# High and low parts of the weighted sums made straight from PSUM, in two operations, in a fused two-layer kernel

## The reference, cut to what matters

```python
qz_u = qz @ ternary_factor_u.T * SCALE          # 16 channels of rank 64
qz_v = qz @ ternary_factor_v.T * SCALE
message_F = jnp.einsum('bcsr,bctr->bcst', qz_u, qz_v)
qh = jax.nn.sigmoid(message_F / REG_H)
qh_v1 = jnp.einsum('bcst,bctr->bcsr', qh, qz_v)
qh_v2 = jnp.einsum('bcst,bcsr->bctr', qh, qz_u)
...
message_G = (qh_v1 @ ternary_factor_u + qh_v2 @ ternary_factor_v) * SCALE
```

## Time and profile before

| | |
|---|---|
| median of 3 runs | 1738.5 us (1736.36 to 1742.24) |
| the profiled execution's own time | 1739.22 us |
| its span, first to last instruction | 1737.4 us |
| PE busy | 1578.7 us, 91% |
| DVE busy | 887.0 us, 51% |
| ACT busy | 826.6 us, 48% |
| granted TensorE clock, mean | 0.975 |

### The profile page before, as it was taken

One profiled execution on the slowest core, in us unless ns is written; L12 is line 12 of the kernel. 1 busy time (PEld: TensorE's weight loads), 2 busy tenths in 40 slices (PEclk: granted clock), 3 DMA queues, 4 the chain that ended last, 5 costly groups with the idle time before them and its releaser, 6 DMA issues.

```text
span 1737.4 us, 26600 instructions
## 1 busy us (share of the span) xinstructions
PE 1578.7 (91%) x8452; PEld 860.5 (50%) x8452; DVE 887.0 (51%) x1632; ACT 826.6 (48%) x1697; POOL 58.1 (3%) x45
## 2 busy tenths in 40 slices
PE   3399699999999899999999999999998999999977
PEld 1377564444445444454445444544555445544544
DVE  7868743334544454445443545445444544454447
ACT  2136235555555454545544554455554555455531
POOL 5000400000000000000000000000000000000000
PEclk9699799999999999999999999999999999999998
DMA  6002000000000000000000000000000000000000
GB/s 187 1 6 69 19 1 1 1 1 1 1 1 1 8 1 2 1 9 1 1 1 8 1 1 1 8 1 1 1 1 9 1 2 1 9 1 1 1 7 6
DMA packets 19945, 16.23 MB, mean 9 GB/s; under 512 B 1512, under 2 KB 18024, under 8 KB 19656
## 3 DMA queue, kind: packets, MB, share of 16 engines
q1 hardware_dynamic: 19448, 12.30, 2.6%
q0 software_dynamic: 336, 1.97, 0.3%
HBM read 9.94 MB, written 2.10 MB: 7 GB/s over the span
## 4 chain that ended last, share of the span: by engine, by line
issue 86%; DVE 6%; PE 6%; POOL 1%; DMA 1%; ACT 1%; SPq 0%; DVEq 0%; POOLq 0%; ACTq 0%
PE bank L1028 5%; DVE upper L514 1%; DMA x_all<-in_x 1%; DVE arena L734 0%; DVE arena L574 0%; DVE small L573 0%; DVE arena L740 0%; DVE upper L629 0%; DVE upper L627 0%; DVE upper L636 0%; DVE upper L638 0%; ACT arena L862 0%; DVE upper L625 0%; DVE upper L623 0%; DVE arena L732 0%
## 5 line engine op out<-in xcount | busy, mean ns | idle before, releaser
L952 ACT ACTIVATE arena<-bank 128x512 f32<-128x512 f32 x512 | 264.2, 602 | 205.4 <-PE bank L1028 205.2
L862 ACT ACTIVATE arena<-bank 128x512 f32<-128x512 f32 (+6 forms) x243 | 137.8, 585 | 337.3 <-PE bank L1165 183.1
L1028 PE MATMUL bank<-arena 128*64 128x512 f32 (+2 forms) x1280 | 282.2, 545 | 6.6 <-DVE arena L784 6.6
L952 ACT ACTIVATE th_high<-bank 128x512 f32<-128x512 f32 x512 | 264.5, 604 | 46.8 <-PE bank L1028 45.8
L682 DVE TENSOR_SCALAR arena<-bank,sums 128x512 f32<-128x512 f32 x128 | 96.1, 751 | 337.7 <-PE bank L1028 337.5
L1028 PE MATMUL bank<-th_high,arena 128*64 128x512 f32 x1024 | 247.9, 605 | 0.0
L1028 PE MATMUL bank<-u_parts,v_parts 64*128 64x512 f32 x1536 | 214.6, 409 | 16.7 <-ACT arena L952 11.3
L1028 PE MATMUL bank<-v_parts,u_parts 64*128 64x512 f32 (+1 forms) x1568 | 221.1, 408 | 0.0
L1028 PEld LDWEIGHTS bank<-v_parts,u_parts 64*128 64x128 f32 (+1 forms) x1568 | 140.2, 184 | 70.8 <-issue 45.8
L1028 PEld LDWEIGHTS bank<-u_parts,v_parts 64*128 64x128 f32 x1536 | 134.7, 184 | 79.7 <-issue 38.9
L938 ACT ACTIVATE arena<-bank 128x512 f32<-128x512 f32 x130 | 77.8, 598 | 174.3 <-PE bank L1028 128.2
(11 more groups left out here) (179 smaller groups left out, 1718.0 us busy)
## 6 DMA issues: line engine op xcount, KB each, us to landing
x_all<-in_x SPq DMA_DIRECT2D x4, 512.0 KB, 12.5
upper<-in_we SPq DMA_DIRECT2D x8, 256.0 KB, 2.7
arena<-upper SPq DMA_DIRECT2D x16, 128.0 KB, 2.5
out<-x_all SPq DMA_DIRECT2D x8, 256.0 KB, 2.3
arena<-in_e POOLq DMA_DIRECT2D x1, 1216.0 KB, 8.4
arena<-in_wi POOLq DMA_DIRECT2D x1, 576.0 KB, 8.6
uT_w<-in_uT SPq DMA_DIRECT2D x1, 512.0 KB, 7.9
vT_w<-in_vT SPq DMA_DIRECT2D x1, 512.0 KB, 6.1
```

What stands on the lines that cost most here:

```text
L862: return nc.scalar.activation(dst, src, ACT.Copy)
L952: nc.scalar.activation(th[n % TH_SLOTS], f_bank[n % F_BANKS][:], ACT.Tanh, scale=0.5 * FACTOR_SCALE ** 2).then_inc(s_th, 1)
L1028: return nc.tensor.matmul(out, lhsT, rhs, start=start, stop=stop)
```

## The change

Both parts are now made from `o_bank` itself. One operation adds `sums` and writes the high part to `o_hl`; a second reads `o_bank` again, adds `sums`, subtracts the high part and writes the low part. `o_s`, `parts_of_o` and the semaphore `s_ol` are gone (the place of `o_s` in the arena stays empty). `s_oe` is now incremented by the second operation. For o = 0 the call has moved from unit 2 to unit 3 of DVE's list; for o = 1 it stays at unit 6. `project` waits on `s_oe`.

```diff
             def evac_o(g, j, o, some_before):
 
+                total = sums[:, o, j % 2:j % 2 + 1]
                 dve.wait_ge(s_out, g * 8 + 4 * (o + 1))
                 if some_before:
-                    dve.wait_ge(s_ol, g * 2 - 1 + o)
-                nc.vector.tensor_scalar(o_s[:, o], o_bank[:], sums[:, o, j % 2:j % 2 + 1], None, ALU.add)\
+                    dve.wait_ge(s_prep_full, prep_index(g, 0) + 1)
+                nc.vector.tensor_scalar(o_hl[:, o, 0], o_bank[:], total, None, ALU.add).then_inc(s_oh, 1)
+                dve.wait_ge(s_oh, g * 2 + o + 1)
+                nc.vector.scalar_tensor_tensor(o_hl[:, o, 1], o_bank[:], total, o_hl[:, o, 0], ALU.add, ALU.subtract)\
                   .then_inc(s_oe, 1)
-
-            def parts_of_o(g, o, some_before):
-
-                dve.wait_ge(s_oe, g * 2 + o + 1)
-                if some_before:
-                    dve.wait_ge(s_prep_full, prep_index(g, 0) + 1)
-                nc.vector.tensor_copy(o_hl[:, o, 0], o_s[:, o]).then_inc(s_oh, 1)
-                dve.wait_ge(s_oh, g * 2 + o + 1)
-                nc.vector.tensor_tensor(o_hl[:, o, 1], o_s[:, o], o_hl[:, o, 0], ALU.subtract).then_inc(s_ol, 1)
...
                     for u in range(UNITS):
-                        if u % TB == TB - TOGETHER:
+                        if u == TB - TOGETHER + 1 or u == UNITS - TOGETHER:
                             evac_o(g, j, u // TB, second or j)
-                        if u == TB:
-                            parts_of_o(g, 0, second or j)
...
-                        if u == UNITS - 1:
-                            parts_of_o(g, 1, second or j)
...
             def project(g, j):
 
                 pe.wait_ge(s_prep_free, prep_index(g, 0))
-                pe.wait_ge(s_ol, g * 2)
+                pe.wait_ge(s_oe, g * 2)
```

More of the change, by code:

```diff
@@ L253, in build @@
         th_low = take(TH_SLOTS // 2, T)
-        o_s = take(2, T)
+        at[0] += 2 * T
         gT = take(T)
@@ L299, in build @@
         s_f, s_th, s_out, s_oe = sem("scores_full"), sem("tanh_done"), sem("unit_done"), sem("o_evacuated")
-        s_oh, s_ol = sem("o_high_ready"), sem("o_low_ready")
+        s_oh = sem("o_high_ready")
         s_lf, s_la, s_ld = sem("l1_bank_full"), sem("l1_emptied_by_act"), sem("l1_emptied_by_dve")
```

## The result

| | before | after |
|---|---|---|
| median | 1738.4 us (1736.4 to 1742.2, 4 runs) | 1802.4 us (1799.6 to 1802.9, 4 runs) |
| span of the profiled execution | 1737.4 us | 1797.5 us |
| PE busy | 1578.7 us, 91% | 1579.2 us, 88% |
| DVE busy | 887.0 us, 51% | 837.9 us, 47% |

The account below looks back on a forecast made before the run. PE sets the pace, busy 175.7 of 184 us a batch; new waits for `o_bank` cost 70.1 us in seven batches + 2.7 in the first - 0.4 at the end = 72.4, on 1739.2: 1811 us, range 1786 to 1828.

Parts of the forecast that it names:

- The operations.: On DVE, high part 751 ns and low part 0.75 us instead of 1866 ns for each o; the saving hides entirely.
- The place.: For o = 0, behind the layer 1 step and split of u, PE waits at unit 4: 9.29 us a batch.
- L656's start + 2.28 us: When PE can start unit 4: 0.61 + 0.79 + 0.75 us, then 0.13 from DVE's end to PE.
- The restart, 0.09 us.: After each wait PE loses the overlap of its weight load with the matmul before: 0.72 us a batch.
- Pair 4, 2.38 us.: PE's wait at unit 4 in pair 4 of a loop batch, the longest of the eight: 2.38 us.
- No later wait.: Removed parts at units 4 and 7 and the new semaphore waits cost nothing, since all are met before.
- The o = 1 side.: Bank freed 1.67 us after L682's start, against 2.05 us in the tightest case; 0.38 us left, nothing lost.
- The first batch.: Without layer 1, a wait of 0.25 us, 0.34 with restart, in each of 8 pairs: 2.7 us.
- The clock.: Rival: more PE idle time lowers the clock; a tenth of the loop at half clock, 1940; within larger delays, 6%.
- not slower: Rival: `o_bank` is free before PE arrives at unit 4, only 0.4 us gained at the end: 1738.8; 4%.
- faster, by DVE's work: Rival: DVE's throughput sets the end, so up to its 46 us of saved busy time would go: 1693; 2%.
- Only the scans count: Rival: quicker release and restart; pairs 0, 3, 5, 7 and first batch lose nothing, 39 us in all: 1778; 8%.

Follow-up runs that it names:

- back_to_unit2: The changed kernel with its two operations for o = 0 put back to unit 2 of DVE's list: 1738.0 us, ratio 0.9991.
- move_only: The kernel before, with its three operations, and only the emptying for o = 0 moved from unit 2 to unit 3: 1763.3 us, ratio 1.0142.
- v_behind_scores_old: The kernel before, with only PE's product for the next v moved behind the scores of units 6 and 7: 1701.7 us, ratio 0.9784.
- behind_l1_step: The changed kernel with the two operations for o = 0 at unit 2, between the layer 1 step and the split of u: 1760.1 us, ratio 1.0133.
- behind_v_split: The changed kernel with the two operations for o = 0 one place further back, at unit 4 behind the split of v: 1922.1 us, ratio 1.105.
- v_behind_unit3: The changed kernel, operations for o = 0 at unit 3, with PE's product for the next v behind the scores of units 6 and 7: 1816.6 us, ratio 1.044.

## Why the prediction was right

The direction, the mechanism and the size hold: 1802.4 us measured, in the range of 1786 to 1828, for 1811 forecast. Point by point:

- *The operations.* 748 and 751 ns, as taken (751 and 750). DVE saved 49 us, and it was worth nothing, which back_to_unit2 shows.
- *The place.* The pairs come in the order forecast, 4, 1, 2, 6, 7, and pairs 0, 3 and 5 last; the seven batches are alike. That place and second operation only add up once the margin is spent is shown by back_to_unit2, move_only and the changed kernel together.
- *0.61 us from L656 to the high part.* It was that again in every pair of the loop. The 5 us more by the rule that the prediction quotes are not there. The prediction left out how the same section of the Trainium skill ("VectorE: DVE Perf Modes", section "The DRAIN you can't avoid") goes on: a next operation that is not held starts earlier, which is what the rows here show, 0.61 us after the start of one of 0.69 us.
- *L656's start + 2.28 us.* It was 2.20: PE starts 0.06 us after the low part ends, not 0.13. I had read the latency from one row where PE waited for the projection. 64 x 0.08 = 5 us too much.
- *The restart, 0.09 us.* It doesn't exist at this place: the delay of PE's start in pair 1 is 1.80 us, which is 981.14 + 2.20 - 981.53 = 1.81 without it, and the group behind takes 1.94 us as before. The 0.07 us that a wait costs beyond its recorded idle time are already in such a difference of two starts. 6 us too much. With the latency that is 11 us too much.
- *Pair 4, 2.38 us.* It was 1.85 on PE, 1.92 as a delay. The gap from the end of the scan to the split of u had been 0.58 us in the kernel before and is 0.21 now, as in pair 2. The longer gap is found in the two kernels that keep the three operations in their old places, before and v_behind_scores_old; of the seven others six, move_only and back_to_unit2 among them, have 0.21, and in behind_l1_step the two operations stand in the gap. So the move alone takes it away, and so do the two operations alone; why the longer gap was there the runs don't say (rows below the list). Past the two terms above that is 0.38 us a batch, and pair 3, counted like pair 5, another 0.09: 3 us too much.
- *No later wait.* Wrong by a little: the split of v behind the two operations makes PE 0.20 us late in pair 0, 1.5 us in all. behind_l1_step, with 0.55 us at the same place, makes its releaser visible.
- *The o = 1 side.* Nothing lost; within a batch no distance from the weighted sums of unit 6 to those of the next unit 0 grew.
- *The end.* From the last weighted sums to the projection 3.67 us instead of 4.07, the 0.4 us forecast.
- *The first batch.* 1.3 us lost instead of 2.7, by the same two terms.
- *The clock.* The rival was given a place in a few per cent of "larger delays", priced as a tenth of the loop. It did happen, but twice, for 3.3 us. The prediction had looked at the busy share of a whole batch; the clock of batch 4 was 1.00, and what fell, fell behind single waits. With the longer waits of behind_v_split and v_behind_unit3 it fell 21 and 11 times, for 33 and 17.5 us.

The split of u in pair 4 of batch 4, in the kernel before and in back_to_unit2:

```profile
1047.60 0.43 DVE L655 CAST u_parts<-arena 128x512 fp32r<-128x512 f32 x1 [0.58 <-PE bank L1028]
```

```profile
1045.78 0.43 DVE L655 CAST u_parts<-arena 128x512 fp32r<-128x512 f32 x1 [0.21 <-ACT arena L928]
```

The sum closes: 72.4 - 11 - 3 + 1.5 + 3.3 = 63 us, against 64 measured and 62.5 in the trace between the first and the last weighted sums. The mechanism was right; that the number came within 9 us is in part luck, since the two terms that were left out, 4.8 us, hid a third of the 14 us that were too much.

Of the rivals, "not slower" and "faster, by DVE's work" are excluded by the 64 waits and by back_to_unit2. "Only the scans count" described move_only, not the change: there pairs 0, 3, 5, 7 and the first batch lost nothing, and the loss was 25 us. move_only frees the bank 0.79 us sooner than the change does, and a sooner release is what that rival had supposed.

## What to carry to other kernels

An operation that frees a buffer should be judged by its place in its engine's list before its own length: here 0.8 us more of it cost nothing ahead of two other tasks and 39 us behind them. The margin between the release and the next user, read pair by pair from the timeline, priced the move here to within 0.16 to 0.26 us in seven pairs of eight and to 0.55 us in the other, each time too high. The 49 us of busy time saved on an engine that waits half of the time said nothing about the result. Once the bounding engine waits for such a release, a better order of its own ahead of the wait gains nothing, and the same 37 us that a better order of PE brings in one kernel vanish in the other.

## What the runs showed of the hardware

- The granted TensorE clock fell to its lower level behind single waits of PE of 1.85 to 2.8 us for `o_bank`, inside a stretch in which PE was otherwise busy, and the following eight matmuls took 2.5 to 3.6 us instead of 1.94. In the changed kernel it happened behind two of seven equal waits of 1.85 us; in behind_v_split not behind any of the seven waits of 2.91 us, but behind each of 2.77, 2.81 and 2.68 us. It also happened behind waits of 1.5 to 2.5 us for the tanh between two batches, at 8 of 54 places.
- A scalar_tensor_tensor with PSUM, an SBUF scalar and an SBUF tensor took 751 ns for 128x512, the same form with a constant scalar 691: the 60 ns of an SBUF scalar are the same as on a tensor_scalar.
- From the end of the DVE operation to PE's matmul that waited for it there were 0.06 us at unit 4, in all 64 pairs of the changed kernel, and 0.15 us before the last projection, in both kernels. What makes the difference was not tried.
